# A GRU scan written out group by group, with the loads split before and beside it, and a shorter scale for the double normalisation

## What is computed

```python
x = x + _layernorm(_L0_attn_ref(_layernorm(x), ...))   # layernorm, GRU over the 512 steps (H = 256), projection, + input
x = x + _layernorm(_L0_ffn_ref(_layernorm(x), ...))    # 8 experts by low-rank adapters, top 1, relu, projection
x = x + _layernorm(_L1_attn_ref(_layernorm(x), ...))   # attention, 16 heads, causal, with silu gate
x = x + _layernorm(_L1_ffn_ref(_layernorm(x), ...))    # gated feed-forward with int weights

def step(h, xt):                                       # one GRU step: 512 of them, each needs the one before
    r = sigmoid(xr_t + h @ w_hr.T + b_hr)
    z = sigmoid(xz_t + h @ w_hz.T + b_hz)
    n = tanh(xn_t + r * (h @ w_hn.T + b_hn))
    return (1.0 - z) * n + z * h
```

## Time and profile before

| | |
|---|---|
| median of 3 runs | 1810.33 us (1808.54 to 1812.36) |
| the profiled execution | 1817.01 us, its span from first to last instruction 1815.3 us |
| granted TensorE clock, mean of the span | 0.656 |
| busy: PE, PEld | 1396.6 us (77%), 1028.5 us (57%) |
| busy: DVE, ACT, POOL | 1207.8 us (67%), 697.1 us (38%), 456.6 us (25%) |
| 68,193 instructions | 27,370 matmuls, 5,761 on DVE, 2,426 on ACT, 872 on POOL |

### The profile page before, as it was taken

One profiled execution on the slowest core, in us unless ns is written; L12 is line 12 of the kernel. 1 busy time (PEld: TensorE's weight loads), 2 busy tenths in 40 slices (PEclk: granted clock), 3 DMA queues, 4 the chain that ended last, 5 costly groups with the idle time before them and its releaser, 6 DMA issues. The chain is left out here.

```text
span 1815.3 us, 68193 instructions
## 1 busy us (share of the span) xinstructions
PE 1396.6 (77%) x27370; PEld 1028.5 (57%) x27370; DVE 1207.8 (67%) x5761; ACT 697.1 (38%) x2426; POOL 456.6 (25%) x872
## 2 busy tenths in 40 slices
PE   1588888878878787878787873579889888979667
PEld 1466777767667676766666662235545544535333
DVE  2477777767767676767776762657677777657265
ACT  1233233222222222222222220127566656656555
POOL 1111211212121121211212123632442442311244
PEclk6555555555555555555555555769999999989889
DMA  7200000000000000000000000691663573570001
GB/s 82 50 4 3 6 5 6 5 17 6 5 7 5 7 17 5 7 5 7 5 16 7 5 5 19 94 132 25 97 81 55 85 107 35 78 90 1 1 12 35
DMA packets 68691, 56.09 MB, mean 31 GB/s; under 512 B 11006, under 2 KB 67734, under 8 KB 68374
## 3 DMA queue, kind: packets, MB, share of 16 engines
q1 hardware_dynamic: 66518, 51.54, 19.3%
q10 hardware_dynamic: 1856, 0.07, 0.1%
HBM read 33.93 MB, written 17.56 MB: 28 GB/s over the span
## 5 line engine op out<-in xcount | busy, mean ns | idle before, releaser
L721 PE MATMUL PS<-GB,W 128*128 128x8 f16 x18432 | 576.2, 168 | 203.1 <-DVE GB L1030 174.9
L721 PEld LDWEIGHTS PS<-GB,W 128*128 128x128 f16 x18432 | 532.8, 104 | 312.0 <-DVE GB L1030 283.2
L1927 DVE TENSOR_REDUCE MX<-PS 128x1 f32<-128x512 f32 (+3 forms) x352 | 223.3, 637 | 163.4 <-PE PS L1655 160.9
L924 ACT ACTIVATE tr<-PS 128x16 f32<-128x16 f32 x512 | 93.7, 183 | 509.4 <-PE PS L721 507.7
L1811 ACT ACTIVATE PT<-PS 128x512 f32<-128x512 f32 (+1 forms) x352 | 194.4, 559 | 168.0 <-PE PS L1671 165.7
L1016 DVE SCALAR_TENSOR_TENSOR u_<-tr,PS 128x16 f32<-128x16 f32 x512 | 87.7, 171 | 129.5 <-PE PS L721 116.7
L926 ACT ACTIVATE tz<-PS 128x16 f32<-128x16 f32 x512 | 93.7, 183 | 194.8 <-PE PS L721 194.8
L1652 PE MATMUL PS<-KS,QS 99*128 99x256 bf16 (+3 forms) x512 | 136.1, 318 | 30.9 <-issue 10.8
L675 POOL TENSOR_TENSOR rt<-mv,eps 128x1 f32<-128x1 f32 x96 | 18.2, 189 | 517.7 <-DVE mv L1041 517.7
L1023 DVE SCALAR_TENSOR_TENSOR zg<-tz,HR 128x16 f32<-128x16 f32 x512 | 92.9, 182 | 79.2 <-ACT tz L926 75.8
L729 PE MATMUL PS<-ones,brow 128*128 128x32 bf16 x1032 | 110.3, 188 | 34.5 <-PEq L207 34.5
(11 more groups left out here) (376 smaller groups left out, 2592.3 us busy)
## 6 DMA issues: line engine op xcount, KB each, us to landing
QS<-q_parts SPq DMA_DIRECT2D x48, 256.0 KB
KS<-k_parts SPq DMA_DIRECT2D x48, 256.0 KB
q_parts<-PQ SPq DMA_DIRECT2D x16, 384.0 KB, 13.3
k_parts<-PK SPq DMA_DIRECT2D x16, 384.0 KB, 13.8
x_steps<-XM SPq DMA_DIRECT2D x32, 64.0 KB, 1.9
out_dram<-X SPq DMA_DIRECT2D x8, 256.0 KB, 2.3
XM<-in_L_attn_x_dram SPq DMA_DIRECT2D x16, 120.0 KB
X<-x_steps SPq DMA_DIRECT2D x3, 512.0 KB, 3.2
```

What stands on the lines that cost most here:

```text
L721: return pe.matmul(bank[:, p, at:at + B], W[:, kc, w:w + P], state[:, part, kc, :], start=False, stop=True, skip_group_check=True)
L924: act.activation(as_states(tr), now(pR), ACT.Tanh, scale=gate_scale).then_inc(hn_tr.sem, 1)
L1927: dve.tensor_reduce(MX[:, g % 2, heads[0]:heads[-1] + 1, NT - 1 - it], p_x[:, k % 2, 0:len(heads) * w].rearrange("p (a w) -> p a w", w=w), ...
```

## The change

1. The scan is written out: all 32 groups are straight code, and UNROLLED and the loop go.
2. The loads are split in three. In the setup block SP issues `s_hh`, `s_ih`, the x rows of groups 0 to 3 for the even steps, and the 13 transfers that the first feed-forward layer needs (`loads_f`). ACT issues the x rows of the odd steps behind its own four. At the start of the scan block SP issues the 14 late transfers (`loads_late`) and the x rows of groups 4 to 11, and when these have landed those of groups 12 to 31.
3. The waits follow: PE and DVE wait for `loads_f` at steps 0 and 2, ACT's wait before the scan goes, PE waits for `loads_late` at step 21, POOL's casts move from step 0 to step 12 and wait for it there, ACT waits for it at step 97. DVE waits for x rows at group 2 and group 10.
4. In the setup block ACT instead of DVE copies the r and z part of the turned `s_hh`. The product `wb` moves ahead of the wait for the scale, the gate biases move ahead of W2 and V2.
5. The product of both scales is taken as one power, (v (1 + eps) + eps^2)^-1/2. `token_scales` goes from 7 instructions with two powers to 2 with one, `row_scales` from 7 to 3 with one power over twice the columns.
6. The last reads of X are for sequence 0 and for 1 to 7 apart, in all four parts. The scan block doesn't wait for them; DVE waits in the attention block, for sequence 0 before its moments and for the rest before those of sequence 1.

```diff
         def token_scales(pool, tmp, step, view, done=0):
 
-            var, tmp, r1, rr, power = view(MV[:, :, 1]), view(tmp[:, :]), view(R1[:, :]), view(RR[:, :]), view(half[:, :])
-            pool.tensor_scalar(tmp, var, EPS, None, ALU.add).then_inc(step, 1)
+            var, tmp, rr, power = view(MV[:, :, 1]), view(tmp[:, :]), view(RR[:, :]), view(half[:, :])
+            pool.tensor_scalar(tmp, var, 1.0 + EPS, EPS * EPS, ALU.mult, ALU.add).then_inc(step, 1)
             pool.wait_ge(step, done + 1)
-            pool.tensor_tensor(r1, tmp, power, ALU.pow).then_inc(step, 1)
-            pool.wait_ge(step, done + 2)
-            pool.tensor_tensor(tmp, r1, r1, ALU.mult).then_inc(step, 1)
-            pool.wait_ge(step, done + 3)
-            pool.tensor_tensor(tmp, tmp, var, ALU.mult).then_inc(step, 1)
-            pool.wait_ge(step, done + 4)
-            pool.tensor_scalar(tmp, tmp, EPS, None, ALU.add).then_inc(step, 1)
-            pool.wait_ge(step, done + 5)
-            pool.tensor_tensor(tmp, tmp, power, ALU.pow).then_inc(step, 1)
-            pool.wait_ge(step, done + 6)
-            pool.tensor_tensor(rr, tmp, r1, ALU.mult).then_inc(step, 1)
-
-        def row_scales(pool, var, tmp, r1, rr, step, done):
-
-            power = half[:, 0:var.shape[1]]
-            pool.tensor_tensor(tmp, var, eps[:, 0:var.shape[1]], ALU.add).then_inc(step.sem, 1)
-            pool.wait_ge(step.sem, done(1))
-            pool.tensor_tensor(r1, tmp, power, ALU.pow).then_inc(step.sem, 1)
+            pool.tensor_tensor(rr, tmp, power, ALU.pow).then_inc(step, 1)
...
+        def row_scales(pool, moments, tmp, scales, step, done):
+
+            n = moments.shape[1]
+            power = half[:, 0:2 * n].rearrange("p (n k) -> p n k", k=2)
+            pool.tensor_scalar(tmp[:, :, 0], moments[:, :, 1], EPS, None, ALU.add).then_inc(step.sem, 1)
+            pool.tensor_scalar(tmp[:, :, 1], moments[:, :, 1], 1.0 + EPS, EPS * EPS, ALU.mult, ALU.add).then_inc(step.sem, 1)
             pool.wait_ge(step.sem, done(2))
-            pool.tensor_tensor(tmp, r1, r1, ALU.mult).then_inc(step.sem, 1)
-            pool.wait_ge(step.sem, done(3))
-            pool.tensor_tensor(tmp, tmp, var, ALU.mult).then_inc(step.sem, 1)
-            pool.wait_ge(step.sem, done(4))
-            pool.tensor_tensor(tmp, tmp, eps[:, 0:var.shape[1]], ALU.add).then_inc(step.sem, 1)
-            pool.wait_ge(step.sem, done(5))
-            pool.tensor_tensor(tmp, tmp, power, ALU.pow).then_inc(step.sem, 1)
-            pool.wait_ge(step.sem, done(6))
-            pool.tensor_tensor(rr, tmp, r1, ALU.mult).then_inc(step.sem, 1)
+            pool.tensor_tensor(scales, tmp, power, ALU.pow).then_inc(step.sem, 1)
...
-        loads_x = signal("loads_x")
-        loads_rest = signal("loads_rest")
+        loads_x = signal("loads_x", 16)
+        loads_f = signal("loads_second_layer")
+        loads_late = signal("loads_late")
+        X_FIRST, X_NEXT = 4, 12
+        x_by_step = x_d.rearrange("b (j t) d -> t b j d", t=GS)
+
+        def load_x(eng, t, first, last, done):
+            eng.dma_start(XM[t * B:(t + 1) * B, first:last, :], x_by_step[t][:, first:last, :]).then_inc(done.sem, 16)
...
+                for t in range(0, GS, 2):
+                    load_x(sp, t, 0, X_FIRST, loads_x0)
...
+            N_F = 5 + FC + 4
+            N_LATE = 14
...
+                for t in range(1, GS, 2):
+                    load_x(act, t, 0, X_FIRST, loads_x0)
                 act.wait_ge(consts.sem, 2)
                 act.activation(warm[:, :], half[:, 0:1], ACT.Tanh).then_inc(warmed.sem, 1)
 
+                for i in range(2):
+                    act.wait_ge(turned.sem, i + 1)
+                    act.activation(whhT[:, i, 0:2 * H], PS[:, i, :], ACT.Copy, scale=0.5).then_inc(kept.sem, 1)
...
-                for i in range(2):
-                    dve.wait_ge(turned.sem, i + 1)
-                    dve.tensor_scalar(whhT[:, i, 0:2 * H], PS[:, i, :], 0.5, None, ALU.mult).then_inc(kept.sem, 1)
...
+                dve.tensor_tensor(wb[:, :, :], s_ih[:, :, :], bet[:, :].unsqueeze(1).to_broadcast([P, 6, D]), ALU.mult).then_inc(bias_v.sem, 1)
...
-                dve.tensor_tensor(wb[:, :, :], s_ih[:, :, :], bet[:, :].unsqueeze(1).to_broadcast([P, 6, D]), ALU.mult).then_inc(bias_v.sem, 1)
-                dve.wait_ge(rstd.sem, 7)
+                dve.wait_ge(rstd.sem, 3)
                 for j, dst in enumerate((YN, YNp)):
                     dve.tensor_scalar(dst[:, :], XM[:, j, :], MG[:, j, 0:1], MG[:, j, 3:4],
                                       ALU.subtract, ALU.mult).then_inc(y_ready.sem, 1)
-                dve.wait_ge(high_w.sem, 1)
-                dve.scalar_tensor_tensor(flat(W2), flat(whhT), S_gru, flat(W1), ALU.mult, ALU.subtract).then_inc(low_w.sem, 1)
-                dve.wait_ge(high_w.sem, 2)
-                dve.scalar_tensor_tensor(V2[:, :], wihT[:, :], S_gru, V1[:, :], ALU.mult, ALU.subtract).then_inc(low_w.sem, 1)
-
...
+                dve.wait_ge(high_w.sem, 1)
+                dve.scalar_tensor_tensor(flat(W2), flat(whhT), S_gru, flat(W1), ALU.mult, ALU.subtract).then_inc(low_w.sem, 1)
+                dve.wait_ge(high_w.sem, 2)
+                dve.scalar_tensor_tensor(V2[:, :], wihT[:, :], S_gru, V1[:, :], ALU.mult, ALU.subtract).then_inc(low_w.sem, 1)
...
-                for j in range(UNROLLED):
+                for j in range(NG):
                     group(j, j % RG)
-                with eng.Fori(0, (NG - UNROLLED) // RG) as i:
-                    for r in range(RG):
-                        group(value(i * RG + (UNROLLED + r)), (UNROLLED + r) % RG)
...
+                for t in range(GS):
+                    load_x(sp, t, X_FIRST, X_NEXT, loads_x)
...
+                sp.wait_ge(loads_x.sem, loads_x.before(sp, GS))
+                for t in range(GS):
+                    load_x(sp, t, X_NEXT, NG, loads_x)
+                sp.wait_ge(loads_late.sem, 16 * N_LATE)
...
-                        for first, n in ((0, B),) if k < NT - 1 else tuple((b, 1) for b in range(B)):
+                        for first, n, back in ((0, 1, x_back0), (1, B - 1, x_back)):
                             sp.dma_start(X[:, k * B + first:k * B + first + n, :],
-                                         xs_d[k * P:(k + 1) * P, first:first + n, :]).then_inc(x_back.sem, 16)
-                sp.wait_ge(x_back.sem, 16 * (NT - 1 + B))
+                                         xs_d[k * P:(k + 1) * P, first:first + n, :]).then_inc(back.sem, 16)
...
-                    if a == 0:
-                        pool.wait_ge(loads_rest.sem, 16 * N_REST)
+                    if a == 12:
+                        pool.wait_ge(loads_late.sem, 16 * N_LATE)
...
-                            pe.wait_ge(loads_rest.sem, 16 * N_REST)
+                            pe.wait_ge(loads_f.sem, 16 * N_F)
                         if i == 9 and o == 0:
                             pe.wait_ge(casts.sem, casts.value(pe, 0, 2))
                         if i == 5 and o == 0:
+                            pe.wait_ge(loads_late.sem, 16 * N_LATE)
...
-                act.wait_ge(loads_rest.sem, 16 * N_REST)
...
-                        if isinstance(j, int) and j == 0:
-                            dve.wait_ge(loads_x.sem, 16 * GS)
+                        if j + 2 in (X_FIRST, X_NEXT):
+                            dve.wait_ge(loads_x.sem, loads_x.before(dve, GS if j + 2 == X_FIRST else 2 * GS))
...
+                dve.wait_ge(x_back0.sem, x_back0.value(dve, NT - 1))
...
+                            if b == 0:
+                                dve.wait_ge(x_back.sem, x_back.value(dve, NT - 1))
```

More of the change, by code:

```diff
@@ L252, in _ @@
             def _(sp):
[L253 to L258, removed]
                 sp.dma_start(s_hh[:, :, :], w_hh_d.rearrange("(c p) k -> p c k", p=P)).then_inc(loads_hh.sem, 16)
                 sp.dma_start(s_ih[:, :, :], w_ih_d.rearrange("(c p) k -> p c k", p=P)).then_inc(loads_ih.sem, 16)
-                x_by_step = x_d.rearrange("b (j t) d -> t b j d", t=GS)
@@ L262, in _ @@
-                for first, last, done in ((0, 2, loads_x0), (2, NG, loads_x)):
-                    for t in range(GS):
-                        sp.dma_start(XM[t * B:(t + 1) * B, first:last, :],
-                                     x_by_step[t][:, first:last, :]).then_inc(done.sem, 16)
-                sp.dma_start(s_out[:, :], w_out_d).then_inc(loads_rest.sem, 16)
-                sp.dma_start(s_wi[:, :, :], wi_d.rearrange("(c p) k -> p c k", p=P)).then_inc(loads_rest.sem, 16)
-                sp.dma_start(s_wo[:, :], wo_d).then_inc(loads_rest.sem, 16)
@@ L269, in _, with row @@
-                sp.dma_start(s_ga[0:E, :], gate_w_d).then_inc(loads_rest.sem, 16)
-                sp.dma_start(s_ga[E:E + E * R, :], lora_a_d.rearrange("e r d -> (e r) d")).then_inc(loads_rest.sem, 16)
+                for t in range(0, GS, 2):
+                    load_x(sp, t, 0, X_FIRST, loads_x0)
+                def row(dst, src):
```

(22 more changed lines are left out.)

67 lines of the change are left out of this document (39 added, 28 removed).

## The result

The changed kernel takes 1751.83 us (median of 4 runs, 1751.36 to 1754.41) against 1811.34 for the kernel before in the same session (1808.54 to 1814.87): a ratio of 0.9659, 95% interval 0.9632 to 0.9687. The forecast was 1746 with a range of 1740 to 1757. The profiled execution has a span of 1749.8 us and took 1751.5.

The account below looks back on a forecast made before the run. Setup was taken as bound by SP's issuing, the scan as a latency chain with loop stalls. Savings of 36.1 + 22.3 + 3.7 + 2.3 = 64.4 us from the median 1810.3 gave 1746, range 1740 to 1757.

Parts of the forecast that it names:

- What bound the setup block: Setup block: bound by SP's issuing; after the change DVE ends it at 23.2 and PE starts at 23.7 instead of 59.17.
- no change: Setup block: x's first rows land at 13.6 as before, with bounds of -1.9 (DVE's floor of 11.7) and +5.0 (18.6).
- the term of 36 us: Head, up to the scan's start: 36.1 us less, 35.5 from PE's earlier start and 0.6 from ACT's wait.
- The loop: Scan groups 8 to 31 written out: 22.3 us less, at 1.950 us a step as in the groups already written out.
- The steps between them last the same: Scan: fewer register instructions per step give nothing; the 22 us are PE's stalls alone.
- Loads beside the scan: Early scan: late loads and x's other rows arrive in time; cost 0, up to 4 us if all comes late.
- its last sentence: Scan: prediction most wrong by a queue or load wait in the first 20 steps, or written-out code stalling beside transfers.
- straight code can't be delivered fast enough: Rival, scan: each of 24 newly written-out groups stalls up to 3.4 us, kernel ends at 1827; chance 0.02.
- Reads and scales: Start of attention: 3.7 us less from the split last reads of X, 2.3 less from shorter POOL scales.
- the rest of the attention takes up the 6.0 us: Rival, attention: its start was not the limit, the q and k trip through DRAM is; 1752; chance 0.05.
- Carrying the offset: Whole kernel: median taken as 6.7 us below the profiled execution after the change too, so 1746 instead of 1752.6.
- the forecast's own range: Whole kernel: 1741 to 1750 with each part within its bounds, chance 0.73; the full range reaches over the first three rivals.

Follow-up runs that it names:

- e4: Changed kernel with all 16 transfers of x's first rows on SP's queue, none on ACT's: 1751.46 us, ratio 0.9666.
- e7: Changed kernel with all loads back in the setup block, nothing issued beside the scan: 1770.2 us, ratio 0.9784.
- e10: Changed kernel with all loads in the setup block and x's rows 4 to 31 in pieces of 112 KB: 1778.17 us, ratio 0.9814.
- e8: Kernel before with the scan's loop written out and nothing else changed: 1782.97 us, ratio 0.9872.
- e3: Changed kernel with the last reads of X in eight pieces, waited for in front of the barrier: 1755.95 us, ratio 0.9697.
- e2: Changed kernel with the attention's token scales by seven instructions and two powers, as before: 1752.49 us, ratio 0.9689.
- e9: Kernel before, unchanged, run again for a second profile: 1813.47 us, ratio 1.0011.
- e1: Changed kernel with groups 11 to 31 in a loop again, 7 turns of 3 groups: 1769.87 us, ratio 0.9789.
- e5: Changed kernel with x's rows 0 and 1 loaded first, rows 2 and 3 behind them, over both queues: 1751.95 us, ratio 0.9667.
- e11: Changed kernel with x's rows 0 and 1 loaded first and rows 12 to 31 issued only in group 4: 1750.01 us, ratio 0.9655.

## Why the prediction was right, and what it missed

**What bound the setup block: right.** With SP's list cut the block ends with DVE, and the steps that led to 23.2 came as written: `wb` in the gap, ACT's `brow` ending at 22.30 (22.4), DVE at 23.03 (23.2). x came at 13.95 (13.6). The choice of "no change" between 11.7 and 18.6 held, and e4 shows that the second queue was no reason for it. e7 and e10 gave 18 and 26 us back and not 36. The difference is x's pace in those programs: PE still starts 0.5 us behind SP's last issue in both, and the time moved with it. So the earlier trace rows was a row of that program, not of the chip, and the term of 36 us holds for this starting point alone.

**The loop: right in kind, 2.7 us too small.** The 22.3 came from the rate of groups 1 to 7 (1.950). But that rate holds longer steps of its own (2.11 and 2.01 in group 3, say), and groups 8 to 31 written out run at 1.942. 25.0 in the profile and 25.4 in e8 are the term's size. "The steps between them last the same" was nearly so: the two longer steps at the end of each looped group went as well, some 3 us. And 8 turns are 7 jumps back.

**Loads beside the scan, "Cost: 0": wrong by 2.3 us**, within the bound of 4 that it was given, but not by the mechanism named, a wait for late data. POOL did stand 7.5 us for the late loads and DVE waited for nothing of it. The loss was 0.7 us where DVE's instructions ran beside POOL's casts, which the prediction did not price, and 1.6 where PE's instructions came late behind x's pieces, which its last sentence names. The rival "straight code can't be delivered fast enough" had this in it and asked for it in every group; it was one stall in four of the eight programs with a burst of large transfers beside the scan, 1.5 to 6.0 us.

**Reads and scales: right**, 4.1 for 3.7 and 2.35 for 2.3; e3 (3.7) and e2 (2.35) give them back. The rival that the rest of the attention takes up the 6.0 us would have XN to the end shorter by that much where attention starts late. The three profiles with the late start (before, e8, e9) took 690.5 us there on average, the nine with both changes 690.7. One profile could not tell it, as this stretch varies by 8 us; together they speak against the rival.

**Carrying the offset: the step that failed.** The sum against the profiled execution gave 1752.6, and the changed kernel takes 1751.8. The prediction then took off the 6.7 us by which that execution lay above its median, as if it would stay. It did not: the profiled run of after is its median within 0.4 us, that of e1 lies 5.4 below its median, and both of the kernel before lie 4 to 6 above, with two of e9's ten runs longer still. A profiled execution is one draw from the spread of its kernel's runs, not a fixed distance from their median. One place of the spread is seen. From XN to the end, code that the change hardly touches, 14 profiles took 686.7 to 695.0 us:

| | before | e9 | after | e1 | e5 | e8 | e10 |
|---|---|---|---|---|---|---|---|
| XN to end, us | 689.8 | 694.4 | 690.0 | 686.7 | 695.0 | 687.4 | 693.0 |

This fits e1's low run and e9's high one. It does not fit the first profile of the kernel before, whose 689.8 is that of the changed kernel; where that execution was longer than its median stays open. Of the 65.5 us between the two profiles the medians show 59.5.

**Luck.** That the sum of 64.4 comes so near the 65.5 of the profiles is partly two misses that nearly cancel: 2.3 us lost in groups 0 and 1 against 2.7 more gained on the loop. And the median stayed in the range, 5.8 us above the forecast, because the range had been reached over the rivals, none of which came as described; the forecast's own range ended at 1750.

## What to carry to other kernels

Take a block apart by who ends it, and list that engine's work to its end: the terms for setup, reads and scales came within 0.4 us of the profile that way. A gain worked out against one profiled execution is a difference of spans; if that execution lies above its median, the range should reach over the offset rather than the forecast carry it. In written-out code look for steps that got longer wherever large transfers run beside it, and see whether the transfers of instructions were held up there.

## What the runs showed of the hardware that was not expected

- The clock is nothing to this scan. In the profile of e5 TensorE was granted 2.4 GHz through all of it, and 384 steps took 743.3 us against 744.05 at 1.2 GHz (page, and window over L925, of e5). One of the step's products takes 168 ns on average at either level, by the pages of the two profiles.

```profile
PEclk9999999999999999999999998589999999989789
```

```profile
273.20:1016.48 743.28, 70.09 (x384) 1.00 0.03 8
```

- Transfers of x of 80 to 120 KB went at 58 to 108 GB/s, at a DMA share of 0.60 to 0.66 each time: more or less time for a 512-byte packet. In two programs profiled twice it was within a tenth; between programs it differed by up to 1.9 times.
- Transfers of x of 80 KB kept PE's instruction transfer from starting for 13 us, and PE stood up to 6.0 us; but with the same transfers beside it, at about the same pace, e1 had no such stall in group 1 (31.35), nor had e2, e4 and e5, where they were faster.
- An instruction of 0.17 us on DVE took 0.68 beside a cast on POOL of 2.17 us, and 0.80 in e4, while e11 shows no stretched one in its scan beside the same cast. All 14 profiles fit one pattern. In 13 of them a DVE instruction of the step with both inputs in SBUF began 0.03 to 0.6 us into that cast, and it ended 0.85 to 0.88 us after the cast's start, whenever it had begun (39.42 + 0.68 = 40.10 against 39.24; in e4 37.79 + 0.80 = 38.59 against 37.73). In e11 the first one came 0.77 us in and was not stretched. The Trainium skill ("SBUF — State Buffer", "SBUF: two separate sides") has DVE, with two inputs in SBUF, fully blocked until a POOL operation that started first ends. By it `GB` would have waited from 39.42 to 41.41; in the trace it was through at 40.10. So there is a wait, but only until some two fifths of the operation are over.
